# New orders for all five engines and new PSUM banks in a two-layer transformer kernel

## The chip, the cores and the metric

The kernel runs on one core of one Trainium2 chip. The metric is the device time of one execution in microseconds (us). Three runs of the kernel before took 231.13, 231.21 and 231.42 us, a median of 231.21 us.

## The reference

The input x has two batches of 512 tokens of 128 features, and there is a context of 154 rows of 96 features for each batch. Four sublayers follow one another, each on the layer norm of x and each added to x:

```python
x = x + cross_attention_0(layernorm(x), ctx)   # 8 heads of 64, softmax over 154 context rows, plus a bias bo
x = x + moe_0(layernorm(x))                    # 16 experts of 64, grouped top-4 routing by sigmoid, a shared expert
x = x + cross_attention_1(layernorm(x), ctx)   # 16 heads of 8
x = x + moe_1(layernorm(x))                    # 8 experts of 256, top-2 of logits + bias, softmax weights, a shared expert
# an expert or shared expert: (silu(x @ w1) * (x @ w3)) @ w2, weighted by token and summed over experts
```

Everything is float32.

## The kernel before

The two batches (b = 0, 1) of 512 tokens are worked on as 4 tiles of 128 tokens. The work is cut into named steps. A step has parts on several engines: for example `h1` is three matmuls of 512 columns on TensorE (PE) and a Silu on ScalarE (ACT). Products of x with weights are done in the fp32r format as three matmuls, L1170, L1171 and L1173 (`product3`): high part by high, low part of the weight by high, high by low part of x. So a step that feeds them (`xT`, `qd`, `hsplit`) is first rounded by ACT, and VectorE (DVE) then takes the rest.

The steps that the prediction speaks of, with the sublayer as their first number (0 to 3) where they have one:

- `kT`, `q`, `vf`, `vs`: keys, queries and values of attention 0. `vf1`, `k1`, `vs1`, `sel`, `qd`, `q1`: the same for attention 1; `place_k1` (ACT) and `place_k1s` (GpSimd, POOL) lay its keys out by head.
- `lnA` (DVE statistics, POOL power and half of the scaling) and `lnB` (ACT, the other half) are the layer norm; `xT` transposes its result (PE L1226, ACT L728, DVE L912).
- `scores`/`score`: PE L1245, DVE maximum L949, ACT Exp L748. `norm`: DVE L956 and POOL L676 and L679. `pT`: transposes L1256, copied by DVE or ACT. `rest`, `pv`, `wo`: the rest of attention 0, `wo` added to x by DVE L988. `bo`: POOL adds the bias.
- `score1`: PE L1384 and DVE maximum L1143; `mT` (PE L1392, ACT L834) turns the maxima, which SyncE (SP) then places by DMA (`place_max`). `expT`: PE L1404 and ACT Exp L845. `expR`: PE L1411 and ACT L852. `rest1`, `pv1`, `od`, `oT`, `onT`, `wo1`: the rest of attention 1.
- `gate`, `route`, `cwT`: the routing. DVE ends it with L1092, PE transposes the weights (L1307), ACT copies them, SP stores them to HBM (`store`) and reads them back spread over partitions (`spread`); POOL then multiplies the Silu of each expert tile by them (`weigh`, L702).
- `h1`, `h3`: the two hidden products, 9 tiles of 128 a batch in sublayer 1 and 18 in sublayer 3. In sublayer 3 DVE multiplies in PSUM (L1110), ACT rounds (`hsplit`, L797) and DVE takes the rest (L1006); `down` is then three matmuls (L1333 to L1335), in sublayer 1 fp32 matmuls (L1326). `res` adds the sum to x, after `ycopy` and `yT` in sublayer 3; `last_down` and `last_res` are the last tile.

Nothing plans at run time. The dictionary `PROGRAM` holds for each of the five engines a string of step names in the order in which that engine does its part of them; the n-th `h1` is always the n-th tile. `order_of` reads it. For PE each name carries the PSUM bank or banks that it writes (`h1.4` writes bank 4; a `down` without a number goes on in the bank of the sum). `bank_uses` derives from these the use count of each of the 8 banks, so the wait of a step for its bank to be read (`wait_bank_free`) is always for the previous use of that bank. All waits are on semaphores, and each engine takes its steps strictly in its order. The intermediate buffers are few: two rounded hidden tiles (`hid_hi`, `m % 2`), seven activation buffers in sublayer 3, two rows of probabilities.

Of the kernel before, what the change touches and what calls it, by code (L numbers as in the profile page):

```python
# [86 lines left out]
def all_steps():  # L87
# [48 lines left out]
    for kind in ("od", "oT"):  # L136
# [40 lines left out]
    "ACT":  # L177
        "kT split lnB kT xT kT kT lnB q xT q split " + 16 * "score " +
        "pT score score pT k1 pT score pT score score split score pv pv score pv pv place_k1 score score " +
        "score score score split score score place_k1 pT score score place_k1 lnB pT k1 pT xT split k1 pT " +  # L180
# [3 lines left out]
        "exp exp expR lnB expR xT exp exp exp qd mT exp exp q1copy q1copy q1copy q1copy expR expR exp exp exp " +  # L184
        "exp split split od exp exp mT exp exp split od expR exp exp exp onT expR mT exp exp exp exp exp expR " +
        "lnB expR exp xT " + 7 * "exp " + "od route od h1 cwT h1 h1 h1 hsplit hsplit h1 onT " + 6 * "h1 " +
        "hsplit hsplit hsplit hsplit lnB h1 hsplit xT h1 hsplit hsplit h1 h1 h1 " + 3 * "h1 hsplit " +
        "hsplit h1 hsplit hsplit route hsplit h1 h1 cwT hsplit h1 h1 hsplit hsplit h1 hsplit h1 ycopy hsplit " +
        "hsplit ycopy h1 hsplit h1 " + 3 * "h1 hsplit " + "hsplit h1 hsplit hsplit h1 " + 3 * "hsplit h1 hsplit " +
# [1349 lines left out]
```

## Time and profile before

| | |
|---|---|
| median of three runs | 231.21 us (231.13 to 231.42) |
| profiled execution, first to last instruction | 229.8 us |
| PE busy | 223.2 us (97%), 1389 matmuls |
| DVE busy | 163.5 us (71%) |
| ACT busy | 155.3 us (68%) |
| POOL busy | 126.4 us (55%) |
| HBM read | 16.08 MB |

The profiled execution is known by its span alone; 1.4 us lie between it and the median. Engine times are unions of instruction times. A matmul of 512 columns shows 390 ns while the next one starts 227 ns after it, so what PE does per time is read from starts, not from busy time.

### The profile page before, as it was taken

The page shows a single profiled execution, that of the slowest core. Times are in us where ns is not written, and L with a number is a line of the kernel's source. Part 1 is how long each engine was busy: PE and PEld are TensorE (multiplying, and loading weights), DVE is VectorE, ACT ScalarE, POOL GpSimd, SP SyncE. Part 2 cuts the span into 40 slices and gives each one's busy share as a digit, 9 for nine tenths or more (in the row PEclk, how much of TensorE's full clock was granted, in tenths as well). Part 3 has the DMA queues.
Part 4 walks back from the last instruction along what each step waited for, and adds up shares of the span by engine and source line. Part 5 has one row for each costly group of instructions (what it writes and reads, how often), then busy time and mean ns, then how long its engine had stood idle before and what let it go on. Part 6 is the DMA issues. An engine that isn't in the chain of part 4 may idle for free.

```text
span 229.8 us, 4648 instructions
## 1 busy us (share of the span) xinstructions
PE 223.2 (97%) x1389; PEld 166.4 (72%) x1389; DVE 163.5 (71%) x480; ACT 155.3 (68%) x378; POOL 126.4 (55%) x127
## 2 busy tenths in 40 slices
PE   7999999999999999999999999999999999999994
PEld 3576765974989898889535563588878887888873
DVE  3689984788667953699948983564857776776874
ACT  2589999986678446662689788876365686645561
POOL 2766742898057927856592107209499400996540
PEclk9999999999999999999999999999999999999999
DMA  6890000000038924800600000037000003600002
GB/s 208 198 303 8 0 3 0 0 3 1 3 93 230 365 105 165 203 0 4 219 3 0 7 0 6 0 82 287 3 0 0 1 3 105 265 0 4 1 0 91
DMA packets 10174, 17.07 MB, mean 74 GB/s; under 512 B 3715, under 2 KB 5540, under 8 KB 9766
## 3 DMA queue, kind: packets, MB, share of 16 engines
q1 hardware_dynamic: 9926, 16.45, 23.1%
q10 hardware_dynamic: 224, 0.32, 0.4%
q8 instruction: 12, 0.20, 0.4%
q14 instruction: 12, 0.10, 0.1%
HBM read 16.08 MB, written 0.62 MB: 73 GB/s over the span
## 4 chain that ended last, share of the span: by engine, by line
PE 83%; ACT 6%; DVE 3%; DMA 2%; SPq 2%; POOL 2%; issue 1%; DVEq 0%; POOLq 0%
PE psum L1170 12%; PE psum L1173 11%; PE psum L1171 11%; PE psum L1326 7%; ACT prob L748 5%; PE psum L1384 5%; PE psum L1333 4%; PE psum L1335 3%; PE psum L1334 3%; PE psum L1435 3%; PE psum L1278 3%; PE psum L1288 3%; PE psum L1404 2%; PE psum L1256 2%; PE psum L1245 2%; DMA ctxT<-in_ctxT 2%
## 5 line engine op out<-in xcount | busy, mean ns | idle before, releaser
L702 POOL TENSOR_TENSOR act_s<-act_s,spread 128x512 f32<-128x512 f32 x35 | 44.4, 1292 | 19.8 <-DMA spread<-cw 13.6
L1170 PE MATMUL psum<-xT_hi,w_hi 128*128 128x512 f32 x108 | 43.9, 406 | 0.0
L1173 PE MATMUL psum<-xT_lo,w_hi 128*128 128x512 f32 x108 | 42.2, 391 | 0.0
L1171 PE MATMUL psum<-xT_hi,w_lo 128*128 128x512 f32 x108 | 42.2, 391 | 0.0
L797 ACT CAST q<-psum 128x512 fp32r<-128x512 f32 x35 | 20.4, 586 | 20.3 <-PE psum L1335 13.7
L1006 DVE TENSOR_TENSOR q<-psum,q 128x512 fp32r<-128x512 f32 x35 | 23.8, 687 | 13.3 <-ACT q L797 13.0
L787 ACT ACTIVATE act_s<-psum 128x512 f32<-128x512 f32 x39 | 23.0, 597 | 12.3 <-PE psum L1173 7.9
L1143 DVE TENSOR_REDUCE neg_max<-psum 128x2 f32<-128x308 f32 x64 | 26.2, 471 | 4.9 <-PE psum L1384 4.7
L702 POOL TENSOR_TENSOR hid<-hid,spread 128x512 f32<-128x512 f32 x13 | 16.6, 1297 | 18.9 <-DMA spread<-cw 14.6
L652 POOL TENSOR_TENSOR rstd<-vareps,minus_half 128x4 f32<-128x4 f32 x8 | 8.1, 1014 | 33.9 <-DVE vareps L907 33.9
L646 POOL TENSOR_TENSOR w_lo<-w_src,w_hi 128x768 fp32r<-128x768 f32 x12 | 21.7, 1830 | 8.9 <-ACT w_hi L717 8.9
L748 ACT ACTIVATE prob<-psum,neg_max 128x154 f32<-128x154 f32 x64 | 24.0, 405 | 1.7 <-DVE neg_max L949 1.0
L1170 PEld LDWEIGHTS psum<-xT_hi,w_hi 128*128 128x128 f32 x108 | 20.3, 188 | 5.5 <-ACT od L860 0.8
L1173 PEld LDWEIGHTS psum<-xT_lo,w_hi 128*128 128x128 f32 x108 | 20.3, 188 | 4.5
L676 POOL TENSOR_TENSOR prob_n<-prob,row_inv 128x1024 f32<-128x1024 f32 x8 | 15.2, 1899 | 13.9 <-DVE row_inv L956 13.9
L1171 PEld LDWEIGHTS psum<-xT_hi,w_lo 128*128 128x128 f32 x108 | 20.4, 188 | 3.3
L845 ACT ACTIVATE probT<-psum 128x512 f32<-128x512 f32 x32 | 16.8, 604 | 3.5 <-PE psum L1404 3.4
L1326 PEld LDWEIGHTS psum<-w,hid 128*128 128x128 f32 x144 | 17.5, 191 | 1.0 <-issue 0.4
L1326 PE MATMUL psum<-w,hid 128*128 128x128 f32 x144 | 18.1, 275 | 0.0
L1384 PE MATMUL psum<-k,q 128*128 128x308 f32 x64 | 16.0, 342 | 0.6 <-DVE neg_max L1143 0.5
L949 DVE TENSOR_REDUCE neg_max<-psum 128x2 f32<-128x308 f32 x32 | 13.5, 463 | 4.2 <-PE psum L1245 4.0
L1384 PEld LDWEIGHTS psum<-k,q 128*128 128x128 f32 x64 | 10.3, 188 | 8.1 <-DVE neg_max L1143 4.6
(171 smaller groups left out, 468.2 us busy)
## 6 DMA issues: line engine op xcount, KB each, us to landing
spread<-cw SPq DMA_DIRECT2D x16, 256.0 KB, 4.4
spread<-cw SPq DMA_DIRECT2D x6, 512.0 KB, 5.5
w_src<-in_w SPq DMA_DIRECT2D x2, 1152.0 KB, 5.3
w_src<-in_w SPq DMA_DIRECT2D x1, 2304.0 KB, 12.4
spread<-cw SPq DMA_DIRECT2D x8, 128.0 KB, 2.9
w<-in_w SPq DMA_DIRECT2D x1, 576.0 KB, 6.9
out<-X SPq DMA_DIRECT2D x4, 128.0 KB, 1.8
wv<-in_wv SPq DMA_DIRECT2D x2, 192.0 KB, 4.8
```

Source lines behind the costliest of these rows:

```text
L646: pool.tensor_tensor(lo, src, hi.bitcast(F32), ALU.subtract).then_inc(lo_of[name], 1)
L702: pool.tensor_tensor(g, g, spread[:, slot, :], ALU.mult).then_inc(weighed, 1)
L748: ins = act.activation(prob[:, r, h, 0:CTX], bank(step)[:, m * CTX:(m + 1) * CTX], ACT.Exp, bias=neg_max0[:, b, t, h:h + 1], accum_out=row ...
L787: moved(act.activation(act_buf(n), bank(step), ACT.Silu), step)
L797: act.copy(hid_hi[:, m % 2, :], bank(("h3",) + step[1:])).then_inc(hid_rounded, 1)
L1006: moved(dve.tensor_tensor(hid_lo[:, m % 2, :], bank(h3), hid_hi[:, m % 2, :].bitcast(F32), ALU.subtract), h3)
L1143: moved(dve.tensor_reduce(neg_max1[:, b, g // 2, 2 * half:2 * half + 2, g % 2, t], bank(step)[:, 0:2 * CTX].rearrange("p (j c) -> p j c", ...
L1170: pe.matmul(dst, w_hi, xT_hi[:, b, :], start=True, stop=False)
L1171: pe.matmul(dst, w_lo, xT_hi[:, b, :], start=False, stop=False)
L1173: return pe.matmul(dst, w_hi, xT_lo[:, b, :], start=False, stop=True)
L1326: ins = pe.matmul(bank(key)[:, t * P:(t + 1) * P], hid[:, n % HIDS, t * P:(t + 1) * P], w2_0[:, i, :], start=(i == 0 and t == 0), stop=las ...
L1384: filled(pe.matmul(bank(step)[:, 0:2 * CTX].rearrange("p (j c) -> p j c", j=2), q1[:, b, g, t * P:(t + 1) * P], k1[:, b, g, 2 * half:2 * h ...
```

## The change

The five strings of `PROGRAM` are replaced. Every engine has the same set of steps as before; 155 of the 377 PE steps, 72 of the 266 of ACT, 110 of the 280 of DVE, 32 of the 85 of POOL and all 34 of SP stand at the same place. Most others move by one to three places. The diff of PE, cut in its unchanged or nearly unchanged middle:

```diff
     "PE":
-        "kT.0 kT.1 kT.0 kT.2 xT.3 vf.1 vf1.4 q.2 q.3 q.4 xT.2 q.3 scores.4.0 scores.3.1 scores.2.5 scores.6.7 " +
-        "scores.0.4 vf.3 q.1 q.2 scores.3.5 scores.6.1 vs.7 pT.2 scores.7.0 pT.4 q.3 pT.2 q.5 pT.6 scores.1.4 " +
-        "pT.7 pT.5 pT.2 k1.6 pT.0 scores.1.7 pT.2 pT.0 pT.5 pT.2 scores.6.4 rest.2.0.1.3 scores.7.5 pv pv pv " +
-        "pv scores.7.0 scores.1.2 scores.3.4 pT.6 wo.5 pT.0 pT.6 wo.1 scores.0.5 pT.3 pT.2 k1.4 vf1.6 vs1.0 " +
-        "pT.5 pT.3 pT.1 pT.2 k1.7 xT.6 k1.2 pT.4 pT.1 pT.6 gate.3 rest.1.6.4.5 pv pv pv pv h1.4 h1.6 wo.5 " +
-        "wo.1 cwT.3 h1.4 h1.3 h3.1 h3.4 h1.7 h3.1 xT.3 h3.0 h1.6 h3.5 gate.3 h3.7 h3.2 down.4 down down h1.1 " +
+        "kT.3 kT.1 kT.6 xT.7 vf.1 kT.5 q.2 q.3 q.4 xT.7 q.2 vf1.6 scores.4.0 scores.3.1 scores.2.5 scores.6.7 " +
+        "scores.0.4 vf.3 q.1 q.2 scores.3.5 scores.6.1 vs.7 pT.2 scores.7.0 pT.4 q.3 pT.5 q.2 pT.6 scores.1.4 " +
+        "pT.7 pT.3 k1.6 pT.0 pT.5 scores.1.7 pT.3 pT.2 pT.5 pT.3 scores.6.4 rest.2.0.1.3 scores.7.5 pv pv pv pv " +
+        "scores.7.0 scores.1.2 scores.3.4 pT.6 pT.5 wo.7 pT.1 wo.0 k1.2 scores.0.5 pT.7 pT.6 vf1.3 vs1.1 pT.7 " +
+        "pT.6 k1.0 pT.5 pT.4 xT.7 k1.2 pT.6 pT.3 pT.4 gate.7 rest.1.6.4.5 pv pv pv pv h1.0 h1.6 wo.1 cwT.7 wo.5 " +
+        "h3.6 h1.3 h1.5 h3.4 h1.7 h3.6 down.3 xT.7 h3.0 h1.1 down gate.5 h3.6 h3.1 down down h1.7 h1.2 h3.6 h1.7 " +
...
-        "score1.6 score1.1 score1.5 score1.2 down h3.4 h3.6 mT.5 down score1.5 score1.4 down score1.5 " +
-        "score1.4 score1.6 down expT.4.5 score1.6 score1.2 expT.1.0 expR.7 expR.3 score1.4 score1.5 score1.6 " +
-        "score1.2 expT.4.1 score1.5 xT.6 score1.2 score1.7 rest1.3.5 score1.0 qd.6 mT.0 expT.1.7 pv1 " +
+        "score1.6 score1.0 down h3.3 score1.4 score1.6 score1.1 mT.5 score1.2 down score1.6 down score1.1 down " +
+        "expT.4.5 expR.2 expR.7 score1.3 score1.4 score1.2 expT.1.0 score1.7 score1.6 score1.5 expT.4.1 score1.3 " +
+        "score1.2 score1.7 score1.0 xT.6 rest1.3.5 qd.4 mT.0 expT.1.7 pv1 q1.1.6.0.4 pv1 score1.1 score1.7 " +
...
-        "score1.7 pv1 score1.2 score1.6 score1.3 expR.1 score1.4 oT.5 expT.7.0 expT.1.2 score1.6 score1.7 " +
-        "onT.5 expT.3.0 score1.1 expR.4 wo1.5 mT.1 wo1.7 rest1.4.6 expT.2.5 pv1 expR.2 expR.5 pv1 expT.2.0 " +
-        "xT.7 expT.5.3 rest1 expT.2.1 expT.7.0 gate.5 h3.2 pv1 pv1 h3.4 oT.0 h1.6 oT.7 cwT.5 h1.1 h3.3 h1.0 " +
-        "h1.5 h1.1 h3.0 onT.5 h3.7 down.1 h1.5 h1.4 h1.2 wo1.5 h1.4 h1.2 h1.6 wo1.4 h3.2 h1.6 h1.4 down down " +
+        "expT.4.0 score1.6 score1.2 score1.3 score1.1 score1.4 score1.7 pv1 score1.1 score1.6 expR.2 score1.4 " +
+        "oT.5 expT.7.0 expT.1.2 score1.3 score1.6 score1.4 score1.7 onT.5 expT.3.0 score1.6 expR.1 wo1.5 wo1.7 " +
+        "mT.1 rest1.4.6 expT.2.5 pv1 expR.7 expR.1 expT.2.0 pv1 xT.7 expT.5.3 rest1 expT.2.1 expT.7.0 gate.5 " +
+        "h1.2 h1.3 pv1 pv1 cwT.0 h1.1 h3.4 h3.7 h3.5 h1.0 oT.6 oT.3 h1.1 h1.0 h1.4 down.1 h3.6 h1.0 onT.7 h1.3 " +
...
-        "down h1.1 down h3.6 down h1.0 down h3.3 down yT.7 down yT.6 last_down.3 yT.7 yT.5 last_down.6 ",
+        "h3.2 down h1.6 down h1.5 h3.3 down h3.5 h1.2 h3.4 down h1.6 h3.2 down down yT.1 h3.6 down down yT.7 " +
+        "last_down.3 yT.5 yT.2 last_down.6 ",
```

Of the other engines, the places that the prediction speaks of:

```diff
     "ACT":
-        "kT split lnB kT xT kT kT lnB q xT q split " + 16 * "score " +
+        "split kT lnB kT kT xT lnB kT q xT split q score score score score score score score score score score " +
...
-        "exp split split od exp exp mT exp exp split od expR exp exp exp onT expR mT exp exp exp exp exp expR " +
-        "lnB expR exp xT " + 7 * "exp " + "od route od h1 cwT h1 h1 h1 hsplit hsplit h1 onT " + 6 * "h1 " +
+        "q1copy expR expR exp exp exp exp od exp exp mT exp exp od expR exp exp exp onT exp expR mT exp exp exp " +
+        "exp expR lnB exp expR xT exp exp exp exp exp split exp route exp od cwT od h1 h1 h1 h1 hsplit h1 h1 " +
+        "hsplit split h1 split hsplit onT hsplit h1 hsplit h1 h1 h1 h1 h1 hsplit lnB hsplit h1 xT h1 hsplit " +
...
     "DVE":
-        "lnA sel lnA xT vf1 q q vf xT " + 9 * "score " +
-        "norm score vf q q score norm score vs score pT score score pT norm score q q pT norm score pT score " +
+        "lnA lnA xT q q xT vf score vf1 score score score score score score score norm score vf score q q score " +
...
-        "norm pT wo pT norm wo score lnA score pT norm pT vf1 pT k1 pT xT pT pT gate route route route route " +
+        "norm score vs score score pT pT norm score score q q pT norm score score pT pT pT score k1 pT score pT " +
+        "score norm score score score score score score norm score pT score score norm pT wo wo lnA score score " +
+        "pT pT norm vs1 vf1 k1 pT pT xT pT k1 gate pT route route route route wo wo h3 lnA sel h3 xT h3 k1 gate " +
...
-        "oT score1 score1 score1 score1 score1 wo1 wo1 lnA xT gate route route oT oT h3 h3 hsplit hsplit h3 " +
+        "score1 score1 score1 score1 score1 wo1 wo1 lnA xT gate route route h3 hsplit h3 oT oT hsplit h3 hsplit " +
...
-        "hsplit h3 hsplit hsplit h3 res res res res last_res last_res ",
+        "hsplit h3 h3 hsplit h3 hsplit h3 hsplit hsplit res h3 res res last_res res last_res ",
     "Pool":
-        "lnA split lnA bo bo split " + 7 * "norm " + "lnA norm place_k1s split split split lnA place_k1s " +
+        "lnA split lnA split norm norm norm norm split bo norm place_k1s bo norm norm lnA norm place_k1s split " +
```

## Rows read from the trace of the kernel before

**Rows 1.** The page: busy time by engine, and the TensorE clock in 40 slices.

```profile
PE 223.2 (97%) x1389; PEld 166.4 (72%) x1389; DVE 163.5 (71%) x480; ACT 155.3 (68%) x378; POOL 126.4 (55%) x127
PEclk9999999999999999999999999999999999999999
```

**Rows 2.** Windows of two stretches: length, busy us (x instructions) by engine, clock, DMA.

```profile
156.00:190.00 34.00, 34.00 (x160) 27.92 (x158) 23.99 (x65) 20.89 (x37) 21.66 (x20) 1.00 0.10 40
190.00:224.00 34.00, 34.00 (x151) 27.80 (x151) 24.25 (x38) 19.68 (x38) 20.34 (x16) 1.00 0.18 63
```

**Rows 3.** Groups by line and shape on PE: busy us, mean ns, idle before.

```profile
L1202 PE MATMUL psum<-wv,ctxT 97*128 97x256 f32 x4 | 1.3, 405 | 0.1
```

**Rows 4.** Timeline of DVE, 9 to 14 us: start, length, line, tiles, shape.

```profile
9.94 0.68 DVE L912 TENSOR_TENSOR xT_lo<-psum,xT_hi 128x512 fp32r<-128x512 f32 x1
13.23 0.68 DVE L920 COPY v<-psum 128x512 f32<-128x512 f32 x1
13.83 0.68 DVE L912 TENSOR_TENSOR xT_lo<-psum,xT_hi 128x512 fp32r<-128x512 f32 x1
```

**Rows 5.** Chain that ended last, 13.5 to 28 us: start, length, what.

```profile
14.64 0.49 DVE neg_max L949
15.16 5.93 ACT prob L748 x31
27.17 0.27 ACT probT L757
```

**Rows 6.** Timeline of PEld (weight loads), at 27.5 us; idle before it in brackets.

```profile
27.48 0.42 PEld L1256 LDWEIGHTS psum<-ident,prob_n 128*128 128x128 f32 x4 [0.33 <-ACT probT L757]
```

**Rows 7.** Timeline of POOL and PE, 45.9 to 51 us.

```profile
46.13 1.02 POOL L652 TENSOR_TENSOR rstd<-vareps,minus_half 128x4 f32<-128x4 f32 x1 [0.34 <-DVE vareps L907]
48.38 1.90 POOL L676 TENSOR_TENSOR prob_n<-prob,row_inv 128x1024 f32<-128x1024 f32 x1
50.92 1.28 PE L1256 MATMUL psum<-ident,prob_n 128*128 128x128 f32 x10 [0.53 <-POOL prob_n L679]
```

**Rows 8.** Timeline of DVE and PE, 109 to 114 us.

```profile
109.42 0.69 DVE L999 TENSOR_TENSOR X<-psum,X 128x512 f32<-128x512 f32 x1
111.62 2.78 DVE L1143 TENSOR_REDUCE neg_max<-psum 128x2 f32<-128x308 f32 x7
111.22 0.43 PE L1384 MATMUL psum<-k,q 128*128 128x308 f32 x2
112.15 0.79 PE L1384 MATMUL psum<-k,q 128*128 128x308 f32 x2 [0.49 <-DVE neg_max L1143]
```

**Rows 9.** Timeline of PE and ACT, 132 to 134.5 us.

```profile
132.82 0.73 PE L1404 MATMUL psum<-q,k 32*128 32x512 f32 x4
133.47 0.94 PE L1384 MATMUL psum<-k,q 128*128 128x308 f32 x2
133.35 1.58 ACT L845 ACTIVATE probT<-psum 128x512 f32<-128x512 f32 x3 [0.41 <-PE psum L1404]
```

**Rows 10.** Timeline of DVE and PE, 144 to 151 us.

```profile
148.51 0.21 DVE L1092 TENSOR_TENSOR cw<-w_un,psum 128x32 f32<-128x32 f32 x1
145.03 0.48 PE L1170 MATMUL psum<-xT_hi,w_hi 128*128 128x512 f32 x1
145.89 1.92 PE L1435 MATMUL psum<-probT,v 128*32 128x512 f32 x16
150.13 0.27 PE L1307 MATMUL psum<-ident,cw 128*32 128x128 f32 x1
```

**Rows 11.** Timeline of ACT, 147.8 to 150.5 us.

```profile
147.88 0.59 ACT L860 COPY od<-psum 128x512 f32<-128x512 f32 x1
148.48 1.28 ACT L787 ACT_TABLE_LOAD   x1
149.90 0.60 ACT L787 ACTIVATE act_s<-psum 128x512 f32<-128x512 f32 x1
```

**Rows 12.** Tile act_s on POOL: ns min/median/max, first and last start.

```profile
L702 POOL TENSOR_TENSOR act_s<-act_s,spread x35: 1267/1295/1316, 68.8 to 222.5; 128x512 f32<-128x512 f32 x35
```

More of the change, by code:

```diff
@@ L152 @@
     "PE":
[24 rows of a table removed]
-    "ACT":
-        "kT split lnB kT xT kT kT lnB q xT q split " + 16 * "score " +
-        "pT score score pT k1 pT score pT score score split score pv pv score pv pv place_k1 score score " +
-        "score score score split score score place_k1 pT score score place_k1 lnB pT k1 pT xT split k1 pT " +
[3 rows of a table removed]
-        "exp exp expR lnB expR xT exp exp exp qd mT exp exp q1copy q1copy q1copy q1copy expR expR exp exp exp " +
-        "exp split split od exp exp mT exp exp split od expR exp exp exp onT expR mT exp exp exp exp exp expR " +
-        "lnB expR exp xT " + 7 * "exp " + "od route od h1 cwT h1 h1 h1 hsplit hsplit h1 onT " + 6 * "h1 " +
-        "hsplit hsplit hsplit hsplit lnB h1 hsplit xT h1 hsplit hsplit h1 h1 h1 " + 3 * "h1 hsplit " +
-        "hsplit h1 hsplit hsplit route hsplit h1 h1 cwT hsplit h1 h1 hsplit hsplit h1 hsplit h1 ycopy hsplit " +
-        "hsplit ycopy h1 hsplit h1 " + 3 * "h1 hsplit " + "hsplit h1 hsplit hsplit h1 " + 3 * "hsplit h1 hsplit " +
-        "ycopy ycopy ",
@@ L191 @@
-    "DVE":
-        "lnA sel lnA xT vf1 q q vf xT " + 9 * "score " +
-        "norm score vf q q score norm score vs score pT score score pT norm score q q pT norm score pT score " +
-        "pT pT score k1 pT score pT score score norm " + 8 * "score " +
-        "norm pT wo pT norm wo score lnA score pT norm pT vf1 pT k1 pT xT pT pT gate route route route route " +
-        "wo wo lnA k1 h3 vs1 xT k1 gate h3 " + 3 * "h3 route " +
-        "h3 h3 h3 route h3 h3 res lnA xT h3 h3 qd h3 h3 score1 score1 score1 score1 score1 h3 " + 7 * "score1 " +
-        "h3 score1 score1 score1 score1 score1 h3 h3 score1 score1 score1 score1 score1 res lnA " + 8 * "score1 " +
-        "xT score1 score1 qd " + 18 * "score1 " + "oT " + 9 * "score1 " +
-        "oT score1 score1 score1 score1 score1 wo1 wo1 lnA xT gate route route oT oT h3 h3 hsplit hsplit h3 " +
-        "wo1 h3 wo1 hsplit h3 h3 lnA hsplit h3 hsplit hsplit hsplit xT h3 h3 gate hsplit hsplit route h3 " +
-        4 * "h3 hsplit " +
-        "h3 h3 hsplit hsplit route hsplit h3 h3 h3 hsplit hsplit h3 hsplit hsplit h3 h3 hsplit h3 h3 hsplit " +
-        "hsplit h3 h3 h3 hsplit h3 hsplit hsplit hsplit h3 h3 hsplit h3 h3 hsplit hsplit h3 hsplit hsplit h3 " +
-        "hsplit h3 hsplit hsplit h3 res res res res last_res last_res ",
@@ L206 @@
-    "Pool":
-        "lnA split lnA bo bo split " + 7 * "norm " + "lnA norm place_k1s split split split lnA place_k1s " +
-        8 * "weigh " + "split split lnA " + 8 * "weigh " +
-        "split split lnA split place_k1s place_k1s split split split lnA split split weigh weigh weigh weigh " +
-        "weigh lnA " + 27 * "weigh ",
[24 rows of a table added]
+    "ACT":
+        "split kT lnB kT kT xT lnB kT q xT split q score score score score score score score score score score " +
+        "score score score score score score pT split score k1 pT score pT score pT score score score pv score " +
+        "place_k1 pv pv pv score score score score score split score score place_k1 pT place_k1 place_k1 score " +
[3 rows of a table added]
+        "place_k1 h1 h1 split mT exp expR exp expR exp exp lnB exp xT exp qd exp mT exp q1copy q1copy q1copy " +
+        "q1copy expR expR exp exp exp exp od exp exp mT exp exp od expR exp exp exp onT exp expR mT exp exp exp " +
+        "exp expR lnB exp expR xT exp exp exp exp exp split exp route exp od cwT od h1 h1 h1 h1 hsplit h1 h1 " +
+        "hsplit split h1 split hsplit onT hsplit h1 hsplit h1 h1 h1 h1 h1 hsplit lnB hsplit h1 xT h1 hsplit " +
+        "hsplit h1 hsplit hsplit h1 route hsplit hsplit h1 h1 hsplit h1 hsplit hsplit cwT hsplit h1 h1 h1 hsplit " +
+        "h1 hsplit h1 hsplit ycopy ycopy h1 hsplit h1 h1 hsplit hsplit hsplit hsplit h1 h1 hsplit h1 hsplit " +
+        "hsplit hsplit h1 hsplit hsplit h1 h1 hsplit h1 hsplit h1 hsplit hsplit ycopy ycopy ",
@@ new lines @@
+    "DVE":
+        "lnA lnA xT q q xT vf score vf1 score score score score score score score norm score vf score q q score " +
+        "norm score vs score score pT pT norm score score q q pT norm score score pT pT pT score k1 pT score pT " +
+        "score norm score score score score score score norm score pT score score norm pT wo wo lnA score score " +
[8 rows of a table added]
+        "route h3 hsplit hsplit route h3 h3 hsplit hsplit h3 h3 hsplit hsplit h3 hsplit h3 h3 hsplit hsplit h3 " +
+        "hsplit h3 hsplit h3 h3 hsplit h3 hsplit hsplit h3 hsplit h3 h3 hsplit h3 hsplit h3 hsplit h3 hsplit " +
+        "hsplit h3 h3 hsplit h3 hsplit h3 hsplit hsplit res h3 res res last_res res last_res ",
@@ new lines @@
+    "Pool":
+        "lnA split lnA split norm norm norm norm split bo norm place_k1s bo norm norm lnA norm place_k1s split " +
+        "place_k1s split lnA weigh weigh weigh weigh weigh weigh weigh split weigh lnA weigh weigh weigh weigh " +
+        "split weigh split weigh weigh weigh split place_k1s lnA split split split lnA split weigh weigh weigh " +
+        "weigh weigh weigh weigh split lnA weigh weigh weigh weigh weigh split weigh weigh weigh weigh weigh " +
+        "weigh weigh weigh weigh weigh weigh weigh weigh weigh weigh weigh weigh weigh weigh weigh ",
@@ L211 @@
     "SP":
-        "store spread spread spread spread spread fetch store spread spread spread spread spread place_max " +
-        "fetch place_max place_max place_max store spread spread spread spread spread store spread spread " +
-        "spread spread spread out out out out ",
+        "store spread spread spread spread spread fetch store spread spread spread spread spread place_max fetch " +
+        "place_max place_max place_max store spread spread spread spread spread store spread spread spread " +
@@ L215 @@
+        "spread spread out out out out ",
 }
```

31 rows, old and new, of the table PROGRAM are left out of this document.

## The prediction

> **What bounds the kernel now.** I read the busy times first. PE is busy for 223.2 us of the 229.8 us span, the other engines for 55 to 71% of it, and the TensorE clock is granted in full (tenths of 9 or more, its 2.4 GHz level) in every slice, so no clock is there to be won [rows 1]. The windows come next: from 156 to 224 us PE has no idle time, and in the later of the two windows 151 matmuls fill 34.00 us, 0.225 us each [rows 2]. An order cannot shorten these: the change leaves the count and the shapes of all matmuls alone. What an order can win is the time in which PE waits. I then looked, matmul by matmul, for starts that come later than the usual distance, and at each for the engine that was late. Five places are worth over 0.2 us, and the sixth is a wait that the new order makes.
>
> The runs' median, 231.21 us, lies 1.4 us above the span of the profiled execution, 229.8 us; I keep this difference and add my sum to the median.
>
> **The change part by part.**
>
> *Start: +0.3 us, later absorbed in part.* `vf1` (b = 0) stood ahead of `q`, in time in which PE would have waited for the low part of x anyway: DVE makes it from 9.94 to 10.62 us [rows 4]. Now it stands behind all four `q`, just ahead of the first `scores`. Its two matmuls have half of the 1.3 us of the group, 0.65 us with their latency [rows 3]; the next step starts some 0.45 us after the first of them (0.25 to 0.65). Another bank for the last `q` (bank 2, read early, for bank 3) gives about 0.15 us back. On DVE the copy of `vf` used to run ahead of `xT` (13.23, then 13.83 us, 0.60 apart); now it is queued between `xT` and the first maximum [rows 4]. So the first maximum comes at about 13.74 + 0.6 + 0.6 = 14.94 instead of 14.64 us by DVE, and at about 14.9 by PE [rows 5]. Behind it ACT runs Exps without a hole from 15.16 to 27.17 us [rows 5], so that +0.3 reaches 27 us in full (0 to +0.5). The kernel before still moved `vf1` through idle time, and that cover is gone.
>
> *27 us: -0.26.* `pT` of tile 2 writes bank 2, which ACT must first copy out (27.17 to 27.44 us); the weight load waits for it 0.33 us, the matmul some 0.26 [rows 5, 6]. In the new order the bank of that copy (5 now) comes up two steps later, behind `k1` and a `pT` on bank 0, some 1 us of work. The wait goes, unless the late Exps bring it back (0 to -0.33).
>
> *51 us: -0.34.* PE idles 0.53 us by the record for the normalisation of the last tile of batch 1 [rows 7]. POOL does it at 48.38, straight after the layer norm, which itself waited 0.34 us for DVE [rows 7]. DVE had put a maximum and a `pT` copy between `wo` and the statistics; now `wo wo lnA` stand together, so POOL can start when it is free. What is late next is POOL itself. Bounds 0 and -0.53; the ACT side of the last tile ends about 0.2 us later than now, behind two `place_k1`, but that still leaves it before the layer norm's end.
>
> *109 to 116 us: -0.8, the largest.* DVE adds the sum of sublayer 1 to x from 109.42 us and does the layer norm's statistics, and only at 111.62 comes to the maxima that empty the banks, seven in 2.78 us, 0.40 each [rows 8]. PE had filled its banks by then: the matmul after those of 111.22 starts at 112.15 (idle 0.49 by the record), the next two are again late by DVE's pace; together about 1.2 us [rows 8]. The new order has both `expR` directly behind the first `expT`, before any `score1`, and two of the later `score1` go to banks emptied long before. That covers 0.6 us with work; two of the new banks hang on ACT's Exps of `expR`, which I expect 0.4 and 0.2 us late. Downstream, `mT` waits for the last maximum of DVE, and DVE's pace does not change, which limits the gain: 116.05 against 116.87 us, -0.8 (0 to -1.2).
>
> *133 us: -0.3.* A `score1` takes bank 7 two matmuls after `expT` filled it (132.82); ACT empties it only from 133.35, and of the 0.94 us of the pair at 133.47 some 0.4 is this wait [rows 9]. The new order has a third `score1` between and ACT no longer has the three splits of `w2_1` in this stretch. Some 0.1 remains. Bounds 0 and -0.6, if the lighter ACT helps its neighbours too.
>
> *148 us: +0.35, a new wait.* `cwT` transposes weights that DVE finishes at 148.51 + 0.21 = 148.72 us, 3.7 us after `gate` has left PE (145.03) [rows 10]. It stood 5.1 us behind it and waited for nothing; now only two `h1` (six matmuls, 1.36 us) and the two `pv1` (1.85 us, 145.89 to 147.74) lie between, with what they lose at their borders 3.4 us [rows 2, 10]. Bounds 0 and +0.7. What it buys, weights spread 1.4 us earlier to POOL, is worth nothing on PE, which did not wait for them.
>
> *148 to 160 us: +0.3.* Behind `cwT` on ACT's queue now stands `od` of batch 1 (it ended at 148.47 before), then the table load of 1.28 us, then the first Silu [rows 11]. Three `h1` are full by then instead of one, and `h3` (tile 0), `hsplit`, both `oT` and `onT` follow each other through ACT and DVE; by adding these up I find banks 4, 6 and 7 free at most 0.15 us before PE wants them. 0 to +1.9, see below.
>
> *At nothing:* the middle of both mixtures of experts, where PE was never late and the closest reuse of a bank of `h1` grows from 1.04 to 1.36 us of PE work (a distance read off the order at the spacing of rows 2); the moved splits of weights, which POOL does 7 us before use; the end, whose adds and DMAs only change places; and the changes of tile shape on PE, of which there is one fewer. ACT's table changes between Exp and Silu are as many as before. Bounds for all these together -0.3 and +0.5.
>
> A rule that speaks against the change: POOL runs beside other DVE work now. The trace has its weighing multiplications between 1267 and 1316 ns, 35 of them, whatever DVE did [rows 12], so nothing is added for this. The Trainium skill ("SBUF — State Buffer", section "SBUF: two separate sides") says that DVE and GpSimd share a port pair under an exclusive lock and that the loser blocks in full for the other's instruction. By it a normalisation could be held up for one DVE instruction, and the sum would be some 0.2 us higher; nothing above rests on it.
>
> **Sum:** +0.3 - 0.26 - 0.34 - 0.8 - 0.3 + 0.35 + 0.3 = -0.75 us, so 230.46; I say 230.4 us.
>
> **The rivals.**
>
> *All gains, no new wait:* the banks of the last stage come free in time and `route` is quicker than PE's four steps. Then +0.35 and +0.3 fall away and 133 us gives more: -1.7, about 229.5 us. For it speaks that DVE and ACT were a third idle there [rows 2]; against it the fixed chain of small DVE instructions of `route`, which nothing shortens.
>
> *Nothing to be measured:* DVE's pace governs the stretch from 109 to 137 us, and what PE gains at 112 it gives back at the next maximum. Then -0.8 and -0.3 are near 0 and the rest cancels: -0.1, about 231.1 us. For it speaks that seven maxima there follow each other without a hole [rows 8].
>
> *Slower, by the opening of the last sublayer:* if `od` ends over 0.15 us later than I reckon, every bank of that chain is late for PE. The full price is the table load and `od` in line, 1.28 + 0.59 = 1.9 us [rows 11] in place of the +0.3: +0.85, about 232.1 us. Against it speaks that PE has several `h1` to do in between.
>
> **How the numbers follow.** Two results of this kernel within 0.2% (0.46 us) cannot be told apart. The forecast (229.9 to 230.75) has 0.45, all gains 0.18, nothing 0.20, slower 0.17. Faster by over 0.2%, below 230.75: 0.62; within: 0.21; slower: 0.17. The range leaves out the ends of both outer cases: 229.2 to 231.9 us.
>
> **What would show it.** At 14.64 us the first maximum 0.3 later and ACT's Exps with it; no wait of PE for ACT at 27 us; PE's wait for POOL at 51 us down to about 0.2 to 0.35; no matmul of L1384 idle for DVE for 0.49 us at 112; and L1307 of the last sublayer held for DVE, right after the second `pv1`. The prediction is wrong if PE waits in the 40 us behind 148, or if the gains at 51 and 112 us are there and the end is not earlier.

## The result and the profile after

The changed kernel takes 233.17 us (median of 6 runs, 232.65 to 233.57), the kernel before 231.62 us on the same chips (6 runs). The ratio is 1.006, with a 95% interval of 1.0043 to 1.0077: slower by 0.6%, which is 1.4 us, and 1.55 us by the two medians. The prediction was 230.4 us with a range up to 231.9, so sign and range were both wrong. It had started from 231.21 us, the median of three runs; six give 231.62. The rest of the distance is the change itself: -0.8 us forecast, +1.55 measured.

The profiled execution of the changed kernel spans 230.8 us against 229.8. Its time is 232.65 us, 1.85 us above its span, and this distance is 1.8 to 1.9 us in every run here, of both kernels. By this the execution profiled before was one of about 231.65 us, and my distance of 1.4 us came from a median and an execution that did not belong together.

The view that explains most is the windows (length, then busy us and instructions of PE, its weight loads, DVE, ACT and POOL, the granted clock, DMA). First the changed kernel, then the kernel before, 60 to 90 and 90 to 109 us (a line of the changed kernel has a number one higher than the same line before, L1171 for L1170):

```profile
60.00:90.00 30.00, 29.60 (x185) 25.76 (x184) 19.43 (x81) 16.46 (x33) 14.10 (x16) 1.00 0.55 170
90.00:109.00 19.00, 18.98 (x127) 16.48 (x126) 14.31 (x30) 12.34 (x22) 16.66 (x15) 1.00 0.35 82
156.00:190.00 34.00, 34.00 (x163) 28.11 (x163) 26.96 (x74) 22.96 (x43) 24.64 (x22) 1.00 0.09 34
190.00:224.00 34.00, 34.00 (x152) 27.89 (x150) 23.42 (x36) 19.31 (x35) 20.27 (x16) 1.00 0.18 63
```

```profile
60.00:90.00 30.00, 30.00 (x190) 26.76 (x189) 20.10 (x81) 17.75 (x33) 16.91 (x20) 1.00 0.52 169
90.00:109.00 19.00, 19.00 (x135) 16.93 (x135) 14.71 (x32) 11.04 (x19) 14.01 (x11) 1.00 0.33 86
```

From 156 us on PE is busy throughout, as before [rows 2]. But in sublayer 1, where PE of the kernel before has no idle time, it now starts 185 matmuls in 30 us where it started 190. I read where the time goes from the starts of PE's steps. After some steps both kernels have done the same set of steps on PE; there the difference of the starts of the next one is what the changed kernel has lost so far:

| next step (before or after) | kernel before, us | lost so far, us | change in the stretch |
|---|---|---|---|
| `vs` | 21.24 | -0.08 | |
| `pT` of tile 2 or `k1` | 27.48 | -0.32 | -0.24 |
| `pT` of tile 3 | 30.12 | -0.08 | +0.24 |
| `k1` of group 3 | 49.69 | +0.28 | +0.36 |
| `pT` of the last tile | 50.92 | -0.22 | -0.50 |
| `xT.1.1` or `down.1.0.0` | 67.04 | -0.11 | +0.11 |
| `down.1.1.0` | 90.73 | +0.85 | **+0.96** |
| first `expT` | 109.31 | +1.34 | **+0.49** |
| `xT` or `score1` of tile 3 | 113.82 | +0.79 | -0.55 |
| `score1.1.3.2.1` | 133.47 | +0.92 | +0.13 |
| `mT` or `wo1` | 136.28 | +0.46 | -0.46 |
| `gate.3.0` | 144.11 | +0.62 | +0.16 |
| `h1.3.0.4` | 152.99 | +0.89 | +0.27 |
| `h3` 3.1.0 | 190.94 | +0.82 | -0.07 |
| last `yT` | 225.78 | +0.78 | -0.04 |
| last output landed | 229.42 | +0.99 | **+0.21** |

The waits that I had named went (27, 112, 133 us) or shrank (at 51 us 0.2 of 0.7 us is left), and the one that I had added came (148 us). Three places in bold, all of them "at nothing" in the prediction, cost 1.66 us and decide the sign.

These are two executions. The others kept here show how far to trust the table. At the start executions of one kernel differ by more than the 0.08 us in the first row: `vs` starts at 21.04 to 21.80 us in the fourteen traces with the changed opening (mean 21.37) and at 21.09 to 21.61 us in the five with the old one (21.32). The middle of sublayer 1 is another matter. From the last `pv` of attention 0 to `down.1.1.0`, the first row in bold, PE takes 33.97 to 34.01 us in all fourteen traces with the old order, and 35.10, 35.71, 35.90 and 36.19 us in the four with the changed order unedited there. So the loss of 1.1 us in this execution is the smallest of four, and the largest is 2.2. From there to the first `expT` the old order takes 18.55 to 18.58 us in eight of eleven traces and up to 19.06 in the others, the changed one 18.81 to 19.06 in the same four.

**The wait at 69 us.** The changed order issues `down` of the first two tiles of batch 0 at 66.9 and 70.2 us (`down.1.0.0` and `down.1.0.1`); they stood at 71.8 and 72.7. The first tile is the shared expert and needs no weights of the routing, the second does. The timeline of PE, POOL, DVE and SyncE's queue (start, length, idle before it in brackets) of the changed kernel:

```profile
69.42 0.40 PE L1174 MATMUL psum<-xT_lo,w_hi 128*128 128x512 f32 x1
70.21 1.13 PE L1327 MATMUL psum<-w,hid 128*128 128x128 f32 x8 [0.39 <-DVE hid L1109]
67.98 2.53 POOL L703 TENSOR_TENSOR act_s<-act_s,spread 128x512 f32<-128x512 f32 x2 [0.43 <-DMA spread<-cw]
69.37 0.69 DVE L1109 TENSOR_TENSOR hid<-psum,act_s 128x512 f32<-128x512 f32 x1 [3.30 <-POOL act_s L703]
61.95 0.52 SPq L591 DMA_DIRECT2D cw<-cwT  x1
64.46 5.64 SPq L609 DMA_DIRECT2D spread<-cw  x9
```

Read it backwards. `down.1.0.1` waits for the product on DVE (70.06), this for POOL's weighing (69.27), this for the routing weights, which SyncE stores at 61.95 and reads back spread from 64.46 us. So PE waits for a round trip through HBM. In the kernel before the same product (DVE at 70.75) was ready 1.30 us before its `down`, the second step of the group that starts at 71.84:

```profile
63.38 0.52 SPq L590 DMA_DIRECT2D cw<-cwT  x1
65.22 6.31 SPq L608 DMA_DIRECT2D spread<-cw  x10
68.79 1.29 POOL L702 TENSOR_TENSOR act_s<-act_s,spread 128x512 f32<-128x512 f32 x1 [0.96 <-DMA spread<-cw]
70.75 0.68 DVE L1108 TENSOR_TENSOR hid<-psum,act_s 128x512 f32<-128x512 f32 x1
71.84 2.84 PE L1326 MATMUL psum<-w,hid 128*128 128x128 f32 x24
```

In the changed kernel it is 0.15 us, as in every trace here in which PE waits at this place. The round trip starts 1.43 us earlier than before, but its first reads only 0.76 us: they follow the start of the store after 1.83 to 1.86 us in the fourteen traces with the old order and after 2.51 to 2.77 us in the six with the changed one. Why the store takes longer there no run shows.

Another profiled execution of the same kernel (after_again below) had the first spreads land later, and its wait was twice as long (`down.1.0.1` 1.83 us after the start of the step ahead of it, which needs 0.68; 1.25 in the execution above):

```profile
71.07 1.13 PE L1327 MATMUL psum<-w,hid 128*128 128x128 f32 x8 [0.97 <-DVE hid L1109]
68.83 2.52 POOL L703 TENSOR_TENSOR act_s<-act_s,spread 128x512 f32<-128x512 f32 x2 [1.00 <-DMA spread<-cw]
60.00:90.00 30.00, 28.89 (x182) 25.12 (x182) 19.64 (x82) 16.34 (x31) 13.20 (x14) 1.00 0.53 163
```

PE idle was 0.00, 0.40 and 1.11 us in these 30 us. The profiled execution is the best of six, 0.5 us below the median, and over this stretch it is the quickest of the four traces: the four stretches above belong to executions of 232.65, 233.36, 233.48 and 234.22 us, in the same order. (The Trainium skill, "DMA: Bandwidth & Descriptors", section "Anatomy of one DMA — SWDGE (gpsimd) path", gives a transfer that GpSimd issues a fixed cost of about 2 us, most of it the receipt of the last write. Here SyncE issues the store, and small as it is it took 2.50 us to landing in the one execution and 2.76 in the other.)

**The end.** DVE's last additions, changed kernel and kernel before:

```profile
226.72 0.42 DVE L979 TENSOR_TENSOR X<-psum,X 128x256 f32<-128x256 f32 x1 [0.32 <-PE psum L1354]
227.24 0.42 DVE L971 TENSOR_TENSOR X<-psum,X 128x256 f32<-128x256 f32 x1
227.58 0.41 DVE L979 TENSOR_TENSOR X<-psum,X 128x256 f32<-128x256 f32 x1
228.09 0.42 DVE L971 TENSOR_TENSOR X<-psum,X 128x256 f32<-128x256 f32 x1
```

```profile
225.95 0.76 DVE L978 TENSOR_TENSOR X<-psum,X 128x256 f32<-128x256 f32 x2 [0.32 <-PE psum L1353]
226.62 0.74 DVE L970 TENSOR_TENSOR X<-psum,X 128x256 f32<-128x256 f32 x2
```

In the old order `res res last_res last_res` an addition starts 0.33 us after the one before, overlapping its end; in `res last_res res last_res` each L971 needs the L979 just ahead of it and starts 0.51 us behind it. From the start of PE's last step, `last_down`, to DVE's end it is 1.71 instead of 1.34 us.

The other places, changed kernel:

```profile
26.45 0.87 PE L1257 MATMUL psum<-ident,prob_n 128*128 128x128 f32 x6
48.16 1.90 POOL L677 TENSOR_TENSOR prob_n<-prob,row_inv 128x1024 f32<-128x1024 f32 x1
50.70 0.52 PE L1257 MATMUL psum<-ident,prob_n 128*128 128x128 f32 x3
112.95 3.17 DVE L1144 TENSOR_REDUCE neg_max<-psum 128x2 f32<-128x308 f32 x8
149.10 0.21 DVE L1093 TENSOR_TENSOR cw<-w_un,psum 128x32 f32<-128x32 f32 x1
149.46 0.27 PE L1308 MATMUL psum<-ident,cw 128*32 128x128 f32 x1 [0.25 <-DVE cw L1093]
```

No wait for ACT at 27 us [rows 6]; the normalisation on POOL starts 0.22 us earlier and `pT` with it [rows 7]; DVE's maxima run without the hole that they had [rows 8]; `cwT` waits for DVE [rows 10].

### The profile page after: what moved, and what is told of

Its sections match the earlier page's. It is cut to its first block and busy times, and to the rows that moved or that the text cites. A ratio compares the mean times of both kernels' runs of the same rounds, so it can differ in the third digit from the quotient of the medians.

```text
span 230.8 us, 4650 instructions
## 1 busy us (share of the span) xinstructions
PE 224.1 (97%) x1389; PEld 166.4 (72%) x1389; DVE 164.2 (71%) x480; ACT 154.9 (67%) x378; POOL 126.4 (55%) x127
## 5 line engine op out<-in xcount | busy, mean ns | idle before, releaser
L1171 PE MATMUL psum<-xT_hi,w_hi 128*128 128x512 f32 x108 | 43.8, 406 | 0.0
L1171 PEld LDWEIGHTS psum<-xT_hi,w_hi 128*128 128x128 f32 x108 | 20.3, 188 | 4.6 <-issue 1.0
L846 ACT ACTIVATE probT<-psum 128x512 f32<-128x512 f32 x32 | 17.6, 601 | 3.2 <-PE psum L1405 3.2
L1111 DVE TENSOR_TENSOR psum<-psum,act_s 128x512 f32<-128x512 f32 x20 | 13.7, 694 | 3.8 <-ACT act_s L788 3.2
```

The source lines that it names most:

```text
L846: moved(act.activation(probT1[:, n % 2, j, :], bank(("expT",) + step[1:]), ACT.Exp, scale=HEAD_SCALE1), ("expT",) + step[1:])
L1171: pe.matmul(dst, w_hi, xT_hi[:, b, :], start=True, stop=False)
```

## The experiments

Each median stands beside that of the kernel before on the same chip. Stretches taken over from a kernel are in its orders and banks on all engines. Where such a stretch meets the rest I had to choose an order of my own, a seam.

**tail_back** and **tail_fwd**: the changed kernel with the old end, and the kernel before with the new one.

```diff
     "DVE":   (tail_back; tail_fwd is the reverse in the kernel before)
-        ... res last_res res last_res
+        ... res res last_res last_res
```

> The changed kernel with one pair exchanged in DVE's order: its last four are again res res last_res last_res (changed kernel: res last_res res last_res). Theory A, every loss sits where the traces show it: the last DVE addition ended 1.585 us after the start of PE's last transpose group in the kernel before and 1.960 us in the changed one, because each last_res waits for the result of the res just ahead of it. Then this kernel is 0.37 us faster than the changed one, some 1.2 us above the kernel before instead of 1.55. Rival B, the output's DMAs hide it (the last one landed only 0.99 us later while the last addition ended 1.15 us later): 0 to 0.2 us faster than the changed one.

> The kernel before with one pair exchanged in DVE's last four, res last_res res last_res as in the changed kernel. Theory A: each last_res waits for its res (0.09 us apart instead of overlapping by 0.08), 0.37 us slower than the kernel before. Rival B, the output's DMAs hide it: within 0.15 us of the kernel before.

Measured: tail_back 233.06 against 231.91 us (1.0044, 1.003 to 1.0059); tail_fwd 232.15 against 231.88 (1.0012, 0.9994 to 1.003). The medians alone can't tell 0.2 from 0.4. The traces can: in all twenty, DVE's end is 1.34 or 1.35 us behind the start of `last_down.1` with the old end and 1.71 or 1.72 with the new one, but the last output lands 3.39 to 3.41 and 3.60 to 3.62 us behind it. So the new end costs 0.20 us, the upper edge of rival B of tail_back: the third output goes 0.15 us earlier, and the last, issued 0.33 us later, then takes 0.12 us less.

**mid_back**, **only_109**, **best1**: the changed kernel with 57.5 to 109 us of the kernel before; the kernel before with 109 to 145 us of the changed one; and the changed one with both mixtures of experts of the kernel before.

```diff
+ mid_back:  changed | before 57.5-109 | changed
+ only_109:  before  | changed 109-145 | before
+ best1:     changed | before 57.5-109 | changed 109-145 | before
```

> The changed kernel with the stretch from the last pv of attention 0 to the last down of sublayer 1 (57.5 to 109 us) in the orders and banks of the kernel before, on all engines. Theory A, the loss is local: over this stretch the changed kernel lost 1.57 us on PE (0.23 ahead at 57.5 us, 1.34 behind at 109.7), so this kernel is 1.4 to 1.6 us faster than the changed one and stands within 0.3 us of the kernel before. Rival B, what PE loses in one stretch is made up where the next one waits for DVE anyway (109 to 116 us): then the gain of the changed order there shrinks with it, and this kernel is only 0.8 to 1.0 us faster than the changed one. Rival C, the difference between the kernels is not in the middle: under 0.4 us faster.

> The kernel before with the stretch of attention 1 alone (109 to 145 us) in the orders and banks of the changed kernel. Theory A: the traces show the changed kernel catching up 0.72 us between 109.7 and 145 us (0.55 by 116 us, 0.54 at 133 to 138 us, less 0.2 at 129 to 131 and 0.2 at 142), so this is 0.7 us faster than the kernel before. Rival B, it caught up only because it came late and DVE's pace is fixed in this stretch: 0 to 0.3 us faster than the kernel before.

> The changed orders up to 57.5 us and from 109 to 145 us, those of the kernel before in the two mixtures of experts (57.5 to 109 us and from 145 us to the end, the tail included). Theory A, stretches add up: 0.23 and 0.72 us, so 0.95 us faster than the kernel before, about 2.5 us faster than the changed one. Rival B, the stretch of attention 1 catches up only what was late: 0.2 to 0.5 us faster than the kernel before.

Measured: mid_back 231.34 against 231.91 us (0.9972, 0.996 to 0.9984), faster than both kernels; by the two ratios it is 0.9%, 2 us, under the changed kernel. Theory A holds: the loss is in this stretch. Its windows from 60 to 109 us are those of the kernel before, and behind 109 us it catches up as the changed kernel did, although it came to 109 us level with the kernel before:

```profile
60.00:90.00 30.00, 30.00 (x190) 26.76 (x189) 19.62 (x82) 18.26 (x33) 16.85 (x20) 1.00 0.55 168
90.00:109.00 19.00, 19.00 (x135) 16.97 (x134) 14.85 (x32) 11.02 (x19) 14.01 (x11) 1.00 0.35 86
```

only_109 was 232.25 against 231.91 and best1 232.34 (ratios 1.0014 and 1.0022): both expectations missed. Their traces show 0.71 and 0.72 us won between 109 and 145 us, and then 1.3 us lost at 145 to 148 us, at my own seam: three splits of `w2_1`, two of which the changed kernel has in the last sublayer, fell close together in front of `od` and `route` on ACT, 0.9 us each. For the stretch itself theory A is right by the traces; of the whole kernels nothing follows.

**wait69**, **cwt81**, **pv1late**: three single moves in the changed kernel, with **after_again**, the changed kernel itself, beside them.

```diff
     "PE":  wait69
-        ... down.3 xT.7 h3.0 h1.1 down gate.5 h3.6 h3.1 down down ...
+        ... down.3 xT.7 h3.0 h1.1 gate.5 h3.6 h3.1 down down down ...
     "DVE": wait69
-        ... wo wo h3 lnA sel h3 xT h3 k1 gate ...
+        ... wo wo h3 lnA sel xT h3 h3 k1 gate ...
     "PE":  cwt81
-        ... h3.4 h3.1 cwT.2 h1.5 down down down h1.1 ...
+        ... h3.4 h3.1 h1.5 down down cwT.2 down h1.1 ...
     "PE":  pv1late
-        ... gate.5 h1.2 h1.3 pv1 pv1 cwT.0 h1.1 ...
+        ... gate.5 h1.2 h1.3 h1.1 pv1 pv1 cwT.0 ...
```

> The changed kernel itself, unedited, as the base for the three single edits beside it on the same chip: 1.2 to 1.6 us above the kernel before.

> The changed kernel with two moves at 69 us: down.1.0.1 goes behind gate.1.1, h3.1.0.4 and h3.1.0.5 on PE again, and on DVE the rest of xT.1.1 goes ahead of h3.1.0.1. Theory A: in the changed kernel PE stands still 0.57 us before down.1.0.1, because its input comes over the whole round trip of the routing weights (store 61.95, spread landed 67.2 and 67.8, POOL to 69.27, DVE to 70.06 us), and the layer norm's xT is queued behind it on DVE. Then this is 0.5 to 0.7 us faster than the changed kernel. Rival B, the next tiles of the same chain hold PE instead (POOL makes one tile in 1.29 us): 0 to 0.25 us faster.

> The changed kernel with cwT.1.1 on PE moved from between h3.1.0.8 and h1.1.1.1 to between down.1.0.7 and down.1.0.8. Theory A: one fp32 transpose between fp32r matmuls costs PE 0.44 us there (0.07 before it, 0.28 itself, 0.10 at the next), against 0.03 to 0.11 beside the downs, which are fp32 as well; nothing behind it waits for the weights. Then this is 0.3 to 0.4 us faster than the changed kernel. Rival B, the weights come 2 us later and POOL's first tile of batch 1 with them: no gain or a loss, -0.1 to +0.5.

> The changed kernel with one h1 of sublayer 3 moved ahead of the last two pv1, so that cwT.3.0 comes behind three h1 and the two pv1 on PE and not behind two. Theory A: the second pv1 of the pair took 1.36 us to the next step instead of 0.97 because cwT.3.0 waits for the end of route on DVE (149.31 us); with 0.7 us more work ahead the wait goes, 0.3 to 0.4 us faster than the changed kernel. Rival B: the wait is only handed on, because the copies of od on ACT and the transposes behind them start that much later: within 0.15 us of the changed kernel.

Measured: after_again 233.44, wait69 234.34, cwt81 234.83, pv1late 233.77 us, the kernel before 231.64. None is faster than after_again in the median.

wait69: in the three runs with a full clock 233.05 us, 0.4 less than after_again; in the three others 235.3 (below). PE lost its idle time in front of `down`, was 0.92 us ahead at `gate.1.1`, and gave 0.74 back at once, because `h3` wants bank 6, which DVE empties only with the next weighed tile:

```profile
71.73 0.50 PE L1171 MATMUL psum<-xT_hi,w_hi 128*128 128x512 f32 x1 [0.56 <-DVE hid L1109]
```

So not `down` alone: every `h3` bank of this stretch hangs on POOL and the round trip (rival B). cwt81: `cwT` beside the `down` saved 0.23 us, about as theory A said, but the weights of batch 1 now came late, and PE lost 1.5 us from 97 to 108 us, first here:

```profile
97.38 1.13 PE L1327 MATMUL psum<-w,hid 128*128 128x128 f32 x8 [0.35 <-DVE hid L1109]
95.17 2.50 POOL L703 TENSOR_TENSOR act_s<-act_s,spread 128x512 f32<-128x512 f32 x2 [1.65 <-DMA spread<-cw]
```

pv1late: the second `pv1` took 0.97 us to the next step instead of 1.36, so the wait of 0.39 was there and went; from `oT` to the fourth `h1` behind it PE then lost 0.7 us. Rival B, with more than it said.

**half_a**: the changed kernel with 57.5 to 90.7 us of the kernel before.

```diff
+ half_a:  changed | before 57.5-90.7 | changed
```

> The changed kernel with the orders and banks of the kernel before from 57.5 to 90.7 us only, the half of sublayer 1 that works on batch 0. Theory A, the round trip of the routing weights: the changed order calls down.1.0.1 at 69 us with its input 0.15 us old in every trace, and stood still 0.57 us there in one and 1.15 us in another execution; the kernel before has 1.3 us to spare. So 1.2 to 1.7 us faster than the changed kernel, or within 0.3 us of the kernel before, and with less spread. Rival B, the loss is mostly in the second half (90.7 to 109 us, 0.49 us in the two traces) and in the last sublayer: under 0.8 us faster than the changed kernel.

Measured: 233.78 against 231.79 us (1.0092): missed. Up to 90.6 us its trace is level with the kernel before (its `down.1.0.1` has 1.30 us to spare again) and has won 1.9 us on after_again since 57 us, as theory A said; then PE stands still 1.94 us for a bank at my seam. What it shows is the first half alone. The second half's share, 0.49 us in the two first traces, stays open: in only_109 and best2 PE waits 0.5 us at `down.1.1.3` in the old order as well.

**expr_only**, **max_first**, **expr_back**: what makes the gain at 109 to 116 us. The first two are single moves in the kernel before, the third one in best2 (below), whose base on the same chip is best2_again.

```diff
     "PE":  expr_only (and ACT likewise)
-        expT.4.5 score1.6 score1.2 expT.1.0 expR.7 expR.3 score1.4 ...
+        expT.4.5 expR.7 expR.3 score1.6 score1.2 expT.1.0 score1.4 ...
     "PE":  max_first (and DVE and ACT likewise)
-        expT.4.1 score1.5 xT.6 score1.2 score1.7 rest1.3.5 score1.0 qd.6
+        expT.4.1 score1.5 score1.2 score1.7 score1.0 xT.6 rest1.3.5 qd.6
     "PE":  expr_back (and ACT likewise)
-        expT.4.5 expR.2 expR.7 score1.3 score1.4 score1.2 expT.1.0 ...
+        expT.4.5 score1.3 score1.4 score1.2 expT.1.0 expR.2 expR.7 ...
```

> The kernel before with one move: both expR of 109 to 111 us go directly behind the first expT, ahead of two score1 and the second expT, on PE and ACT, on their old banks. Theory A, the cover makes the gain of this stretch (0.55 us in the traces): 0.3 to 0.6 us faster than the kernel before. Rival B, DVE's seven maxima in a row set it, and the gain is by the whole new order and its banks: within 0.2 us of the kernel before.

> The kernel before with the two score1 of 114.3 to 116 us ahead of xT.2.1 and rest1.0.0 on PE, the matching maximum ahead of xT on DVE, and one exp ahead of xT on ACT. Theory A: the gain of the changed order in this stretch is DVE's; its maxima then follow each other at 0.385 us without the hole of 0.33 us in front of the eighth and without the late pair behind xT, so mT comes 0.4 us earlier: 0.3 to 0.5 us faster than the kernel before. Rival B, it needs the banks of the changed order too: 0 to 0.15 us faster.

> best2 itself, unedited, as the base of expr_back on the same chip: 0.4 to 0.8 us faster than the kernel before.

> best2 with the two expR of 110 us back behind the second expT, on PE and ACT, in their new banks; all score1 stay in the changed order and banks. Theory A, my step of the prediction, the expR are the cover without which PE waits for DVE's maxima: 0.3 to 0.6 us slower than best2. Rival B, DVE's row of maxima without a hole makes the gain (the four last score1 ahead of xT and rest1), the cover nothing: within 0.15 us of best2.

Measured: expr_only 231.87 against 231.79 us (0.9997, 0.998 to 1.0014), no gain. Its `expR` on bank 7 waits for DVE's addition of the sum that lay in that bank:

```profile
110.53 0.73 PE L1412 MATMUL psum<-q,k1s 128*128 128x512 f32 x2 [0.36 <-DVE X L1000]
```

max_first 234.44 against 231.88 us (1.0116) and expr_back 236.65 against 231.89, with best2_again at 231.25: both far slower, by new waits for banks and their price on the clock. In expr_back PE first waits for the bank of the first `expR`, then ACT comes to the second `expR` only behind `lnB`, and PE waits for its bank:

```profile
112.53 0.73 PE L1412 MATMUL psum<-q,k1s 128*128 128x512 f32 x2 [1.44 <-DVE neg_max L1144]
114.96 1.14 PE L1385 MATMUL psum<-k,q 128*128 128x308 f32 x3 [1.70 <-ACT rest_exp L853]
```

So the cover by `expR` is worth nothing on the old banks. That the new banks are worth nothing without the cover is not shown: expr_back also brought waits of its own making. The gain of 0.55 us belongs to the set (seen in the traces of the changed kernel, mid_back, best2 and only_109); which member carries how much stays open.

**best2** to **best5**: best2 is mid_back with the old end. best3, best4 and best5 go on from it.

```diff
     "PE":  best3 (and DVE likewise)
-        vf.1 kT.5 q.2 q.3 q.4 xT.7 q.2 vf1.6 scores.4.0
+        vf.1 kT.5 vf1.6 q.2 q.3 q.4 xT.7 q.2 scores.4.0
     "PE":  best4 (best5: also the last sublayer of the kernel before)
-        q1.2.6.3.1 down score1.2 score1.5 h3.0 score1.2
+        q1.2.6.3.1 h3.0 down score1.2 score1.5 score1.2
     "ACT":  best5
-        exp exp split split od route od h1 cwT h1 h1 h1 hsplit hsplit h1 onT h1 h1 h1
+        exp exp od route od h1 cwT h1 h1 h1 hsplit hsplit h1 onT h1 split h1 split h1
     "Pool": best5
-        split lnA split split split weigh weigh weigh weigh weigh lnA weigh weigh
+        split lnA split weigh weigh weigh weigh weigh split lnA weigh weigh split
```

> The kernel mid_back (changed orders, but those of the kernel before from 57.5 to 109 us) with DVE's last four in the order res res last_res last_res. Theory A, the tail is the chain of DVE: 0.37 us faster than mid_back, so 0.8 to 1.0 us faster than the kernel before (mid_back was 0.57). Rival B, the output's DMAs hide it: 0.5 to 0.7 us faster than the kernel before.

> best2 with vf1 of batch 0 back in front of the four q, on PE and DVE. Theory A, my step of the prediction: vf1 costs PE some 0.45 us behind q and almost nothing in front, where PE waits for the low part of x (DVE makes it at 9.33 to 10.01 us in the changed kernel): 0.2 to 0.4 us faster than best2. Rival B, the first maxima and ACT's 32 Exps set the pace up to 27 us and the vf1 stands in time that PE has: within 0.15 us of best2.

> best2 (0.3% faster than the kernel before) with h3.1.1.5 ahead of down.1.1.3 on PE, 0.68 us more for POOL's weighing of that tile. In best2's trace PE waited 0.5 us there, its input 0.15 us old; in mid_back, the same order, it did not. Theory A, the round trip of the weights ends late in some executions: 0.2 to 0.4 us faster than best2, so 0.8 to 1.1 us faster than the kernel before, and with less spread. Rival B, the wait moves to the next weighed tile or to the maxima behind it: within 0.15 us of best2.

> best4 with the last sublayer in the orders and banks of the kernel before, two splits of weights placed late as in the changed one. Theory A, in the traces the changed opening of the last sublayer loses 0.3 us at cwT.3.0 and wins 0.15 back: 0.1 to 0.3 us faster than best4. Rival B, what it loses at cwT is made good by earlier weights later on: within 0.1 us of best4, or slower.

Measured: best2 231.17 against 231.79 us (0.9968, 0.9952 to 0.9984) and again 231.25 against 231.89 (0.9976, 0.9964 to 0.9988): the fastest kernel here, 0.6 us under the kernel before and 2 us under the changed one, in two sets of runs. Against mid_back (0.9972) the old end can't be seen in the medians. best3 231.58, 0.4 slower than best2: both theories missed; `vf1` in front of `q` won nothing. best4 231.82: the wait at `down.1.1.3` is gone, and 0.5 us come back at the next `score1`; rival B. best5 233.04: missed, 0.3 us lost at 148 and 0.9 at 158 to 160 us, where my two late splits stand; nothing follows for the last sublayer.

## Why the prediction was wrong, step by step

- *Start, +0.3*: did not come. At `vs` the changed opening is 0.06 us later in the mean of nineteen traces. I had counted `vf1` and overlooked that `sel` leaves DVE in front of the second layer norm: the low part of x is made from 9.33 us, not 9.94 [rows 4]. By best3 the new place of `vf1` was no cost that could be measured.
- *27 us, -0.26*: right and worthless. The wait went (-0.24), and by 30 us it was given back (+0.24), before the next `pT` copies.
- *51 us, -0.34*: the step came, at 0.50 from the point just before it, but the stretch ahead, where `scores`, `k1` and `pT` stand in another order, had lost 0.36. POOL set the end, as I had said ("What is late next is POOL itself"): -0.14 net.
- *109 to 116 us, -0.8*: right in place, 0.55 in size at 113.8 us and 0.45 at `mT`, for which I had forecast it. Of its two reasons, the cover by `expR` and new banks for later `score1`, the first alone gave 0 (expr_only); how the gain divides stays open.
- *133 us, -0.3*: mis-sized, -0.46 from 133.5 to 136.3 us.
- *148 us, +0.35*: right. The pair of `pv1` took 0.39 us longer in the profiled execution, and pv1late removed just that. But then the time was lost behind it: it was no free slack.
- *Opening of the last sublayer, +0.3*: it was -0.07 from 153 to 191 us. The banks came free in time.
- *At nothing* is the step that failed. "the middle of both mixtures of experts, where PE was never late" was argued from where PE had waited, and from the distance between uses of banks; I did not compute when each `down` gets its input. I had bounded all these terms together by +0.5; in sublayer 1 alone it was +0.96 and +0.49 us in the profiled execution, and in three others the first of these was 0.6 to 1.1 larger. mid_back settles where: undoing this stretch alone makes the kernel faster than the one before. Of the 0.96, 0.57 is the wait of `down.1.0.1` for its input at 69 us; about 0.33 is `cwT` between fp32r matmuls, of which cwt81 won back 0.23.
- *At nothing, the end*: "whose adds and DMAs only change places". They depend on each other; +0.20.

The rivals were built from waits that I had found, too. The slower one sat at 148 us, in the wrong mixture of experts, and its 232.1 us, to which I had given 0.17, lay outside my range. The rival "nothing to be measured" was added up wrongly: without -0.8 and -0.3 the terms leave +0.35, about 231.55 us, not -0.1. One of my signs did come true: the gains at 51 and 112 us are there, and the end is not earlier.

## What to carry to other kernels

When an order changes, compute for every moved consumer how old its input was, not where the engine waited: a step with 1.3 us to spare is not free to move 2.5 us forward. Look first at inputs that come over a DMA round trip, because their arrival differs from run to run. At the end of a kernel, put instructions next to each other that do not need each other's results, and count to the landing of the last output. An order, its banks and its neighbours' orders are one thing: of the eleven kernels here that move a single piece, none was measurably faster than its base. mid_back, which moves a whole stretch, was; half_a, only_109 and best5, which move whole stretches too, lost at their seams.

## What had not been expected of the hardware

A PE that waits can pay twice. In expr_back PE was idle for 3.5 of the 6 us from 109 us on, and then the granted clock was at its lower level, 1.2 GHz, for almost all of the 7 us in which it was busy throughout (0.51 of full speed in the mean); likewise, at 0.57, in the profiled execution of half_a, after 1.94 us idle. The windows, expr_back and then half_a:

```profile
109.00:115.00 6.00, 2.51 (x10) 1.12 (x10) 3.37 (x15) 3.62 (x8) 3.35 (x5) 1.00 0.61 210
115.00:122.00 7.00, 7.00 (x32) 3.97 (x33) 3.58 (x8) 2.07 (x4) 5.48 (x7) 0.51 0.00 0
```

```profile
90.00:94.00 4.00, 2.06 (x16) 1.74 (x15) 1.89 (x3) 1.61 (x4) 2.75 (x4) 1.00 0.96 248
94.00:98.00 4.00, 4.00 (x22) 3.31 (x20) 1.98 (x3) 2.54 (x4) 4.00 (x4) 0.57 0.65 144
```

Of the 6.0 us that PE loses in expr_back against best2_again from 109 us to `mT`, 3.4 are lost by the end of the two waits shown above, and the other 2.6 come behind them, mostly under the lower clock. In max_first the clock was 0.57 from 114 to 126 us after only 0.6 us of idle time in the 6 us ahead. And it need not come in every run: half_a ran at a mean clock of 1.0 in four of six executions, and wait69 took 233.0 to 233.5 us in three runs, with a mean clock of 0.998 or more, and 235.2 to 235.5 us in three others, with 0.993. The same order, 2.2 us apart. The profiled execution of wait69 was one of the first kind and shows none of it. What decides is not shown here: after_again had 1.11 us idle between 60 and 90 us and kept the full clock, and tail_fwd, which differs from the kernel before only at the very end, fell to 0.991 and 0.993 in two of its twelve executions.
